# A Fourier-layer tokenizer: scale, shift and gelu moved ahead of the transpose, epsilon as a 33rd column, one power for two chunks

## The reference, cut to what matters

```
h = layer_norm(x @ fc0_w + fc0_b, ln0_g, ln0_b)          # 32 channels per pixel
for i in range(4):
    x1 = spectral_conv(h, w1, w2)                        # rfft2, 12+12 x 12 modes mixed, irfft2
    x2 = einsum('bchw,oc->bohw', h, conv_w[i]) + conv_b[i]
    h = layer_norm(x1 + x2, ln_g[i], ln_b[i])            # over the 32 channels
    if i < 3: h = gelu(h)
h = gelu(h @ fc1_w + fc1_b); h = gelu(h @ fc2_w + fc2_b); h = h @ fc3_w + fc3_b
layer_norm(v) = (v - mean) * rsqrt(var + 1e-5) * g + b
```

## Time and profile before

| what | value |
|---|---|
| median of 3 runs | 9749.03 us |
| profiled execution, device time | 9742.89 us |
| profiled execution, span of its instructions | 9740.8 us |
| PE busy, share of the span | 85% |
| DVE busy | 47% |
| ACT busy | 40% |
| POOL busy | 42%, nearly all of it 1280 powers |
| mean granted TensorE clock | 0.931 |

### The profile page before, as it was taken

The page is one execution under the profiler, slowest core; times in us unless marked ns, Lnnn a source line. Parts: engine busy times, 40 slices in busy tenths (PEclk is TensorE's granted clock), DMA queues, the critical chain, the costliest instruction groups (busy, mean ns, idle before and its releaser), DMA issues. The chain is left out here.

```text
span 9740.8 us, 157193 instructions
## 1 busy us (share of the span) xinstructions
PE 8233.6 (85%) x54638; PEld 5648.8 (58%) x54638; DVE 4556.1 (47%) x8991; ACT 3935.6 (40%) x6803; POOL 4060.7 (42%) x1780
## 2 busy tenths in 40 slices
PE   8888888888888888888888999999986766667667
PEld 5555666666666666666664444444434555555555
DVE  5666455554455554555542222222235555555554
ACT  4444333333333333333335666666651221212212
POOL 7777266663565662666632333333321111111110
PEclk9999999999999998999999999999997878778787
DMA  2222433334333334333432111111110000000000
GB/s 80 89 88 89 156 129 129 128 129 147 128 129 125 129 124 151 129 129 126 129 134 77 36 41 36 41 36 41 36 44 2 2 1 2 1 2 1 2 2 2
DMA packets 568019, 731.26 MB, mean 75 GB/s; under 512 B 450504, under 2 KB 489544, under 8 KB 502216
## 3 DMA queue, kind: packets, MB, share of 16 engines
q1 hardware_dynamic: 567880, 729.71, 22.8%
HBM read 375.13 MB, written 354.45 MB: 75 GB/s over the span
## 5 line engine op out<-in xcount | busy, mean ns | idle before, releaser
L583 POOL TENSOR_TENSOR sb_rstd<-sb_var,sb_minus_half 128x16 f32<-128x16 f32 x1280 | 3697.2, 2899 | 3525.4 <-DVE sb_var L519 3525.4
L516 DVE TENSOR_REDUCE sb_var<-sb_square 128x16 f32<-128x512 f32 x1280 | 873.2, 682 | 1198.9 <-ACT sb_square L455 1193.1
L462 ACT ACTIVATE sb_act_out<-TC,sb_shift,sb_gain 128x512 f32<-128x512 f32 x1280 | 995.0, 777 | 802.1 <-PE TC L331 800.2
L531 DVE COPY sb_pix<-TP 128x512 f32<-128x512 f32 x1024 | 704.8, 688 | 1264.9 <-PE TP L340 1264.3
L455 ACT ACTIVATE sb_square<-H 128x512 f32<-128x512 f32 x1280 | 760.0, 594 | 1180.5 <-PE H L324 1065.7
L311 PE MATMUL H<-sb_conv_block,sb_act_in 128*128 128x128 f32 x8192 | 1054.4, 281 | 64.5 <-DVE sb_unit L524 64.5
L524 DVE TENSOR_TENSOR sb_unit<-H,sb_rstd 128x512 f32<-128x512 f32 x1280 | 882.6, 690 | 419.9 <-POOL sb_rstd L583 412.0
L311 PEld LDWEIGHTS H<-sb_conv_block,sb_act_in 128*128 128x128 f32 x8192 | 970.8, 194 | 127.5 <-DVE sb_unit L524 77.9
L352 PEld LDWEIGHTS M<-sb_table,sb_pix 128*128 128x128 f32 x8192 | 944.6, 194 | 159.8 <-DVE sb_pix L531 156.0
L352 PE MATMUL M<-sb_table,sb_pix 128*128 128x52 f32 x8192 | 977.4, 278 | 3.7 <-DVE sb_pix L531 3.7
L331 PEld LDWEIGHTS TC<-sb_table,sb_unit 128*128 128x128 f32 x5120 | 559.2, 144 | 671.0 <-issue 512.6
(11 more groups left out here) (215 smaller groups left out, 9864.5 us busy)
## 6 DMA issues: line engine op xcount, KB each, us to landing
act_scratch<-sb_act_out SPq DMA_DIRECT2D x256, 1024.0 KB, 3.9
sb_act_in<-act_scratch SPq DMA_DIRECT2D x256, 1024.0 KB, 5.3
spectrum_in<-sb_f_sb SPq DMA_DIRECT2D x512, 78.0 KB, 1.8
sb_x_in<-spectrum_in SPq DMA_DIRECT2D x48, 832.0 KB, 4.2
spectrum_out<-sb_y_sb SPq DMA_DIRECT2D x48, 832.0 KB, 4.4
sb_z_in<-spectrum_out SPq DMA_DIRECT2D x512, 78.0 KB, 5.1
sb_w_raw<-in_w_mix_dram SPq DMA_DIRECT2D x48, 208.0 KB, 4.0
sb_image_in<-in_x_dram SPq DMA_DIRECT2D x64, 96.0 KB, 2.0
```

Source lines behind the costliest of these rows:

```text
L462: e.activation(act_out[q][:, 512 * k:512 * k + 512], TC[:, :], gelu, bias=shift[:, 0:1], scale=gain[:, 0:1]).then_inc(act_ready, 1)
L516: e.tensor_reduce(var[j % 2][:, :], square[j % 2][:, :].rearrange("p (y c) -> p y c", c=C), AX.X, ALU.add).then_inc(var_sum, 1)
L531: e.tensor_copy(dst, TP[:, :].rearrange("p (c x) -> p c x", c=16)).then_inc(pix_ready, 1)
L583: e.tensor_tensor(rstd[j % 2][:, :], var[j % 2][:, :], minus_half[:, :], ALU.pow).then_inc(rstd_ready, 1)
```

## The change

Pass 5 gets functions of its own (`pe_last`, `act_last`, `dve_last`), which hold the old order. Pass 1 and the middle passes get `pe_mid`, `act_mid` and `dve_mid`. In these:

- `square` has 33 columns for each pixel, the 33rd set to epsilon once; the sum over 33 gives var + epsilon, and L519 is gone (in pass 5 too). `var` and `rstd` have four places instead of two.
- GpSimd raises two chunks, 128x32, in one instruction (in pass 5 still one chunk of 128x16).
- DVE applies scale and shift in the pixel layout, in two more 128x512 instructions on `unit`, with `gain_row` and `shift_row` broadcast from SBUF.
- ACT writes gelu of `unit` twice: to `act_px`, which PE transposes, and to `pix` in the order of the forward transform. ACT then copies TC to `act_out`.
- PE's `to_pixels` and DVE's copy from TP are gone. `forward_y` writes TP instead of M[1], and DVE copies it in one instruction instead of two. `pix` is double.

The core of the diff:

```diff
+            def normal(c, k):
+                rows = unit[k % 2][:, :].rearrange("p (y c) -> p y c", c=C)
+                e.wait_ge(rstd_ready, c + 1)
+                at_least(e, pix_ready, c - 1)
+                e.tensor_tensor(rows, H[k][:, :].rearrange("p (y c) -> p y c", c=C),
+                                rstd[k].unsqueeze(2).to_broadcast([128, 16, C]), ALU.mult).then_inc(unit_ready, 1)
+                e.wait_ge(unit_ready, c + 1)
+                e.tensor_tensor(rows, rows, gain_row[:, :].unsqueeze(1).to_broadcast([128, 16, C]),
+                                ALU.mult).then_inc(scaled, 1)
+                e.wait_ge(scaled, c + 1)
+                e.tensor_tensor(rows, rows, shift_row[:, :].unsqueeze(1).to_broadcast([128, 16, C]),
+                                ALU.add).then_inc(affine_ready, 1)
...
+            if back:
+                normal(g0 - 2, 2)
+                normal(g0 - 1, 3)
+            for j in range(4):
+                if front and j == 2:
+                    normal(g0, 0)
+                if front and j % 2 == 0:
+                    variance(j)
+                    variance(j + 1)
+                if front and j == 3:
+                    normal(g0 + 1, 1)
+                if back and j == 3:
+                    spectrum()
...
             def gelus(c, q, k):
+                e.wait_ge(affine_ready, c + 1)
+                at_least(e, tc_ready, c - 1)
+                e.activation(act_px[k % 2][:, :], unit[k % 2][:, :], gelu).then_inc(px_ready, 1)
...
+                e.activation(dst, unit[k % 2][:, :].rearrange("p (x c) -> p c x", c=16), gelu).then_inc(pix_ready, 1)
...
+            for h in range(2):
+                e.wait_ge(var_ready, g0 + 2 * h + 2)
+                e.tensor_tensor(rstd_two[h][:, :], var_two[h][:, :], minus_half[:, :], ALU.pow).then_inc(rstd_ready, 2)
...
+            e.dma_start(gain_row[:, :], g.partition_broadcast(128)).then_inc(layer_in, 16)
+            e.dma_start(shift_row[:, :], b.partition_broadcast(128)).then_inc(layer_in, 16)
```

More of the change, by code:

```diff
@@ L191, in build_tokenizer @@
         act_ready = sem("act_ready")
[L192 removed]
+        scaled = sem("scaled")
+        affine_ready = sem("affine_ready")
+        px_ready = sem("px_ready")
         pix_ready = sem("pix_ready")
@@ new lines, in to_channels, with forward_x @@
+            def to_channels(c, q, k):
+                e.wait_ge(px_ready, c + 1)
+                at_least(e, act_ready, c)
+                for u in range(4):
+                    mm = e.transpose(TC[:, 128 * u:128 * u + 128], act_px[k % 2][:, 128 * u:128 * u + 128],
+                                     const("ident"))
+                mm.then_inc(tc_ready, 1)
+            def forward_x():
+                e.wait_ge(pix_ready, g0)
+                if not front:
+                    at_least(e, f1_ready, 2 * (it - 1))
+                for u in range(2):
+                    for g in range(8):
+                        at = 128 * (8 * u + g)
+                        mm = e.matmul(M[u][:, 52 * g:52 * g + 52], pix[1 - p][:, at:at + 128], const("f1"),
+                                      start=True, stop=True)
+                    mm.then_inc(f1_done, 1)
@@ new lines, in forward_y @@
+            def forward_y():
+                e.wait_ge(f1_ready, 2 * it)
+                at_least(e, f2_ready, it - 1)
+                for i in range(2):
+                    src = f1_sb[:, :].rearrange("p (c i t) -> p c i t", c=16, i=2)[:, :, i, :]
+                    mm = e.matmul(TP[64 * i:64 * i + 48, 0:16 * T26], const("f2"), src, start=True, stop=True,
+                                  skip_group_check=True)
+                mm.then_inc(f2_done, 1)
+            if front:
+                inverse_x()
@@ new lines, in pe_mid @@
+            for j in range(4):
+                three = behind(g0, p, j, 3, front, back)
+                if front and not first and j % 2 == 0:
+                    conv(j)
+                    conv(j + 1)
+                if three:
+                    to_channels(*three)
+                if front and j % 2 == 0:
+                    inverse_y(j)
+                    inverse_y(j + 1)
+                if back and j == 2:
+                    forward_x()
+                if back and j == 3:
+                    forward_y()
@@ L459, in gelus @@
                 e.wait_ge(tc_ready, c + 1)
-                if not last and k == 0:
-                    at_least(e, st_a[p], 16 * P)
-                e.activation(act_out[q][:, 512 * k:512 * k + 512], TC[:, :], gelu, bias=shift[:, 0:1],
+                e.activation(act_out[q][:, 512 * k:512 * k + 512], TC[:, :], ACT.Identity, bias=shift[:, 0:1],
                              scale=gain[:, 0:1]).then_inc(act_ready, 1)
@@ L558, in dve_step, with pool_step @@
             for j in range(4):
[L559 to L562 removed]
+                one, four = (behind(g0, p, j, lag, front, back) for lag in (1, 4))
+                if four and four[2] % 2:
                     copy_heads(four[0])
[L564 to L566 removed]
+                if one and j % 2 == 0:
                     normal(*one)
[L568 removed]
+                if front:
                     variance(j)
[L570 removed]
+                if one and j % 2:
                     normal(*one)
[L572 to L574 removed]
+                if four and four[2] % 2:
                     heads_out(*four)
[L577 removed]
+        def pool_step(e, P, p, front, last):
             g0 = 8 * P + 4 * p
@@ L879, in _ @@
             e.memset(zeros[:, :], 0.0)
+            for p in range(2):
+                e.memset(square[p][:, :].rearrange("p (y c) -> p y c", c=C + 1)[:, :, C:C + 1], EPS)
             e.memset(ones[:, :], 1.0).then_inc(set_up, 1)
@@ L922, in _ @@
             e.wait_ge(set_up, 7)
-            step = lambda P, p, front, *at: pool_step(e, P, p, front)
+            step = lambda P, p, front, back, first, last: pool_step(e, P, p, front, last)
             whole_pass(fori, 0, step, True, False)
```

293 lines of the change are left out of this document (161 added, 132 removed).

## The result

The changed kernel takes 10,620.4 us (median of 4 runs, 10,617.4 to 10,625.9) against 9,749.1 us before; ratio 1.0894, 95% interval [1.0875, 1.0912]. It is 8.9% slower; the prediction was 10,600 us. The profiled execution took 10,617.4 us with a span of 10,615.6, that is 874.8 us more than before.

A forecast was written before the change was run, and what follows sets the result against it. PE was taken to bound pass 5 and nearly the middle passes, a pipeline with POOL longest pass 1. 9743 us plus 352 (pass 1), 472 (middle passes) and 30 (ends) gave about 10,600; range 10,180 to 11,050.

The forecast's parts named there:

- The power: POOL's instruction raising two chunks, 32 columns: taken as 5.6 us, between 5.03 and 5.76.
- Rival 2: On POOL, a 32-column power costs the same as a 16-column one, 2.9 us: total 9160 us; chance 0.09.
- The prices on DVE: DVE: each of the two new 128x512 instructions 0.69 us, the sum with 33 columns 0.70.
- Leg 1: From the end of chunks 2, 3's power to the next power's start, through DVE and ACT: 5.6 us.
- the cycle: Waits around one step, two legs and two powers with DVE standing still behind the first: 20.3 us; chance 0.60.
- Leg 2: From the end of chunks 0, 1's power to chunks 2, 3's: normal 0 and sums 2, 3, 3.5 us.
- The clock in the middle passes: PE falls to 1.2 GHz after a wait; half of 1.8 us, 0.9 a step, making middle steps 21.2.
- The hole: PE's time without work ahead of chunk 0's transposition, after forward_x: some 2.7 us a step.
- Rival 1: New DVE instructions and POOL's power exclude each other: 1.85 us more a step, 22.15; total 10,900; chance 0.24.
- The sum: Whole kernel: pass 1 +352, middle passes +472, ends +30, pass 5, mixing stages and block 0: about 10,600 us.
- ends: Ends of four passes: longer last chains, 22 us, and broadcast loads before the mixing stages, 8: +30.
- upper bound: Power 5.76, new DVE instructions 0.77, full clock loss, steps 21.3 and 22.8 us: +1230, total 10,980.

The follow-up runs named there:

- e12: Changed kernel, but ACT writes the second copy of each chunk in the order it is read, pixel permutation left out: 10,385 us, ratio 1.0639.
- e1: Changed kernel with four powers of 16 columns a step in place of two of 32 in pass 1 and middle passes: 9,225 us, ratio 0.9461.
- e4: Changed kernel with each power over only the first 16 of its 32 columns in pass 1 and middle passes: 9,594 us, ratio 0.9832.
- e8: Changed kernel with ACT's squares 0 and 1 and channel copy ahead of the gelu writes of the chunk normalised last: 10,361 us, ratio 1.0615.
- e2: Changed kernel with DVE's sums of chunks 2 and 3 ahead of normal 0 instead of behind it: 10,344 us, ratio 1.0598.
- e5: Changed kernel with five filler matmuls of 128x512 on PE behind forward_x in the middle passes: 10,499 us, ratio 1.0759.

## Why the prediction was right

- **The power.** Taken at 5.6 us between 5.03 and 5.76; it is 5.43. Rival 2, a power that costs the same for 32 columns, is out.
- **The prices on DVE.** 0.69 taken, 0.692 and 0.692 measured; the sum with 33 columns 0.70 taken, 0.696 measured.
- **Leg 1.** Taken as 5.6, measured 6.44. The path was right (it goes through ACT), the size wrong; this is the one mis-sized term of the cycle, +0.8. Half of it, 0.46, is the order on ACT: the writes were counted 0.5 us apart, and the one behind the strided write starts 0.97 later (500.70 to 501.67). e12 takes 0.45 out. The other 0.35 lies in the four handovers from engine to engine, counted as 0.05, 0.03, 0.03 and 0.08 and measured as 0.12 (DVE still has its spectrum copy), 0.11, 0.17 (the second sum stands behind the first) and 0.14.
- **Leg 2.** Taken as 3.5, measured 3.54.
- **The cycle.** 20.3 taken; 20.84 measured = +0.84 from leg 1, +0.04 from leg 2, -0.34 from two powers. Three runs confirm it in pass 1: e1 takes the standing powers away, and the step falls to 14.8 us where the granted clock is 1.00; e4 shortens both by 2.53, and the step falls by 5.06 to 15.78 in the steps at 2.4 GHz; e8 shortens leg 1 by 0.75, and the step falls by 0.7. The cycle does not say what stands behind it: e4's steps of 20.7 us and e2's path through four engines were not foreseen.
- **The clock in the middle passes.** 0.9 us a step taken as half of 1.8; e5 gives 0.76. The hole was put at 2.7 us and is 2.85. The half was a guess between nothing and 1.8, so that it comes so near is luck. "In pass 1 the clock is free" holds for the total of this kernel, but the clock is at 1.2 GHz for much of it (0.68), and there a bound of 20.7 us lies just beneath the cycle's 20.84 (e4).
- **Rival 1, the lock.** Out: L439 and L442 run beside a power without a wait, and no distance is 22.15 throughout. The Trainium skill, "SBUF — State Buffer", section "Who interferes with whom", lets a DVE instruction with two SBUF inputs and a GpSimd instruction that reads SBUF exclude each other; by that the one at 513.68 would have been held until 518.63. It took 0.69 us, so for this power the measurement decides against the rule. But the trace of before fits the rule for another GpSimd instruction, a TENSOR_TENSOR of 260 columns, and the prediction overlooked it when it said that no row has such a pair. Its own L1501 is one:

```profile
7452.98 0.73 POOL L1697 TENSOR_TENSOR blk_y_sum<-blk_y_sum,blk_dB 128x260 f32<-128x260 f32 x1 [1.90 <-DVE blk_dB L1563]
...
7453.45 0.81 DVE L1501 TENSOR_TENSOR blk_acc<-blk_acc,blk_part 65x512 f32<-65x512 f32 x1
...
7473.09 0.69 DVE L1501 TENSOR_TENSOR blk_acc<-blk_acc,blk_part 65x512 f32<-65x512 f32 x1
```

Of its 112 instances 22 start beside no GpSimd instruction and take 0.69 us; 15 start 0.19 us before the end of such an instruction and take 0.73; 75 start 0.26 us before it and take 0.81. The delay, 0.04 and 0.12 us, is 0.14 us less than what is left of the GpSimd instruction in both, so each further stretch of it is waited out in full. The 774 ns that the prediction read as "slower than its size" are the mean of these three. So the rival deserved its chance, and whether it holds depends on the GpSimd instruction: this one delays DVE, the power does not.
- **The sum.** Pass 1 +352 against 64 x 5.97 = +382; middle +472 against 192 x 2.74 = +526; ends +30 against +25 (392.7 - 382 = 11, 537.2 - 526 = 11, setup 3); pass 5 at 0 against -12; the block at 0 against -46. The last was not seen: the row L1522 stood in the profile of before, with 43.1 us of issue time. Terms off by +84 and -63 nearly cancel, so that the total comes within 21 us is luck; its parts do not.
- **Slips in the working.** The upper bound's step of 21.3 us adds up to 21.0 by its own terms (5.83 + 5.76 + 3.63 + 5.76), 19 us in that total. ACT gains twelve writes a step and gives up four, not eight and four; the 12 us a step given for ACT is right for a gain of eight. The forecast hangs on neither.
